# Latent attention: the value products of both key halves in one run per four heads

## The reference, cut to what matters

```
q = (x @ Wq + bq).reshape(B, S, H, Dh)
latent = x @ Wl + bl
k = (latent @ Wk + bk).reshape(B, S, H, Dh)
v = (latent @ Wv + bv).reshape(B, S, H, Dh)
scores = jnp.einsum('bihd,bjhd->bhij', q, k) * SCALE
attn = jax.nn.softmax(scores, axis=-1)
out = jnp.einsum('bhij,bjhd->bihd', attn, v).reshape(B, S, D)
out = out @ Wo + bo
```

## Time and profile before

| what | value |
|---|---|
| median of 3 runs | 912.23 us (909.99 to 913.12) |
| profiled execution, its own time | 912.18 us |
| its span, first to last instruction | 910.4 us |
| TensorE busy, share of the span | 88% |
| latent stage, turns 0 to 7 | 513.9 to about 661 us of the span |

### The profile page before, as it was taken

One profiled execution on the slowest core, in us unless ns is written; L12 is line 12 of the kernel. 1 busy time (PEld: TensorE's weight loads), 2 busy tenths in 40 slices (PEclk: granted clock), 3 DMA queues, 4 the chain that ended last, 5 costly groups with the idle time before them and its releaser, 6 DMA issues.

```text
span 910.4 us, 22033 instructions
## 1 busy us (share of the span) xinstructions
PE 798.7 (88%) x8648; PEld 535.8 (59%) x8648; DVE 588.9 (65%) x1662; ACT 404.0 (44%) x993; POOL 177.7 (20%) x355
## 2 busy tenths in 40 slices
PE   2579999976599999999985899999959999998997
PEld 1445555535366667668862455555536666667885
DVE  5847878866646776775654566667444677676564
ACT  2435444424244444434431266667614444443443
POOL 6105434521100100000003554331000000000000
PEclk9979999977799999999995599999979999999998
DMA  6000000000000000000002322232000000000000
GB/s 214 0 1 1 2 1 1 2 1 0 0 1 3 2 3 2 2 3 1 1 2 73 101 76 85 84 85 63 2 1 1 3 3 3 2 2 2 2 25 24
DMA packets 13764, 20.01 MB, mean 22 GB/s; under 512 B 1504, under 2 KB 12128, under 8 KB 12256
## 3 DMA queue, kind: packets, MB, share of 16 engines
q1 hardware_dynamic: 13520, 18.43, 6.9%
q10 hardware_dynamic: 144, 0.20, 0.1%
HBM read 14.30 MB, written 4.19 MB: 20 GB/s over the span
## 4 chain that ended last, share of the span: by engine, by line
PE 74%; DVE 11%; issue 5%; ACT 5%; POOL 3%; DMA 1%; DVEq 0%; SPq 0%; ACTq 0%; POOLq 0%
PE bank L1624 8%; PE bank L1696 7%; PE bank L1682 5%; PE bank L1666 5%; PE bank L1631 3%; PE bank L1722 3%; PE bank L1105 3%; PE bank L617 2%; PE bank L1886 2%; PE bank L1126 2%; PE bank L1139 2%; PE bank L1840 2%; PE bank L1827 2%; PE bank L629 2%; PE bank L1835 1%
## 5 line engine op out<-in xcount | busy, mean ns | idle before, releaser
L1422 DVE TENSOR_REDUCE arena<-bank 128x2 f32<-128x512 f32 x128 | 85.1, 688 | 53.4 <-PE bank L1105 53.1
L1243 ACT ACTIVATE arena<-bank 128x512 f32<-128x512 f32 x128 | 74.5, 594 | 51.2 <-PE bank L1126 50.4
L2214 DVE TENSOR_REDUCE arena<-bank 128x4 f32<-128x768 f32 x64 | 61.2, 956 | 32.1 <-PE bank L1666 32.1
L1624 PE MATMUL bank<-arena,w_sb 128*128 128x256 f32 x256 | 75.9, 422 | 1.3 <-ACT arena L1962 1.3
L1983 ACT ACTIVATE arena<-bank 128x768 f32<-128x768 f32 x64 | 51.9, 811 | 44.2 <-PE bank L1688 44.2
L2123 POOL TENSOR_TENSOR arena<-arena,c_sb 128x8 bf16<-128x8 f32 x32 | 9.0, 280 | 286.8 <-issue 249.2
L1682 PE MATMUL bank<-arena 64*64 64x192 f32 (+1 forms) x1024 | 54.9, 308 | 0.4 <-ACT arena L1983 0.4
L1696 PE MATMUL bank<-arena 128*32 128x192 f32 x1024 | 53.9, 328 | 1.6 <-DVE x L2229 1.6
L1624 PEld LDWEIGHTS bank<-arena,w_sb 128*128 128x128 f32 x256 | 46.2, 200 | 14.7 <-ACT arena L1962 2.1
L1105 PE MATMUL bank<-arena 72*128 72x256 bf16 x256 | 52.6, 293 | 1.1 <-DVE arena L1422 1.1
L1126 PE MATMUL bank<-arena 128*128 128x256 bf16 x256 | 49.8, 278 | 0.5 <-ACT arena L1243 0.4
(11 more groups left out here) (297 smaller groups left out, 1793.7 us busy)
## 6 DMA issues: line engine op xcount, KB each, us to landing
arena<-q_dram SPq DMA_DIRECT2D x24, 192.0 KB
arena<-k_dram SPq DMA_DIRECT2D x24, 192.0 KB
w_sb<-w_dram SPq DMA_DIRECT2D x2, 1514.5 KB, 10.3
q_dram<-arena SPq DMA_DIRECT2D x24, 64.0 KB, 2.8
k_dram<-arena SPq DMA_DIRECT2D x24, 64.0 KB, 2.0
x<-x_dram SPq DMA_DIRECT2D x4, 256.0 KB, 4.6
out_dram<-x SPq DMA_DIRECT2D x4, 256.0 KB, 2.3
arena<-arena SPq DMA_DIRECT2D x32, 4.0 KB
```

Source lines behind the costliest of these rows:

```text
L1243: act.activation(a_pT[:, u % (2 * GROUP), :, :].rearrange("p k t -> p (k t)"), bank[2 + u % 2][:, :], ACT.Exp).then_inc(S["p"], 1)
L1422: dve.tensor_reduce(a_mx[:, i % 2, :, u % GROUP], bank[s % 2][:, :].rearrange("p (h k) -> p h k", h=HALVES), AX_X, ALU.max, negate=True).t ...
L1624: ins = pe.matmul(to[:, j * T:(j + 1) * T], w_sb[:, at:at + P], g_zT[b % 2][:], start=True, stop=True)
L2214: dve.tensor_reduce(g_mx[:, s, :, :, i].rearrange("p h j -> p j h"), two_banks(0)[:, :, 0:SPAN].rearrange("p j (h k) -> p j h k", h=HALVES ...
```

## The change

Before, a run stands at every odd step: at steps 1, 5, 9 and 13 the first half of the keys of a group, and two steps later, at 3, 7, 11 and 15, the second half. (A group's runs come five and seven steps after its first head, so those of the last group of a batch stand in steps 1 and 3 of the next turn.) After, both halves stand at steps 1, 5, 9 and 13, one behind the other, and nothing stands at the other odd steps. The products are the same in number and form.

```diff
                     at = b * AH + u - GROUP - 1
-                    if u % 2 == 1 and 0 <= at < B * AH:
-                        values(at // AH, at % AH // GROUP, at % GROUP // 2)
+                    if u % GROUP == 1 and 0 <= at < B * AH:
+                        for k in range(HALVES):
+                            values(at // AH, at % AH // GROUP, k)
```

## The result

The changed kernel takes 924.5 us (median of 4 runs, 922.98 to 925.49) against 912.12 for the kernel before (912.23 in the runs shown ahead, one more was added). The ratio is 1.0137, with a 95% interval of 1.0115 to 1.016. I had forecast 919.6 and a range up to 923.5: the direction was right, the loss of 12.4 us lies outside the range.

A forecast was written before the change was run, and what follows sets the result against it. TensorE's list was taken to set the pace, other engines counting only where it waits. Turn losses of 0.86 + 3.66 + 0.86 + 0.9 + 1.1 = 7.4 us on 912.2 gave 919.6 us, range 914.5 to 923.5.

The forecast's parts named there:

- What a run and a second run cost: On TensorE, a run of `values` taken away frees 0.66 us; a second run right behind another adds 0.43.
- The chains: Within a turn, each second run delays the next chain's start by 0.43 us; freed 0.66 mostly becomes waiting; +1.22 at turn end.
- The sum: Latent stage, turns 0 to 7: 0.86 + 3.66 + 0.86 + 0.9 + 1.1 = 7.4 us lost.
- the three waits: TensorE's waits before `turn_outputs` of step 7, `project_out` and `turn_y`, forecast to grow to about 0.9 to 1.1 us.
- the sentence on the bounds: Latent stage: waits growing to some 0.9 us could cost clock; no row shows longer ones; only a little chance left.
- the prediction's own signs of being wrong: Waits staying at 0.2 to 0.5 us, two runs not following at 0.43, or granted clock leaving 1.00 inside the stage.
- The first: Rival: TensorE keeps the drains saved because chains have slack, 905.1 us; faster, below 909.5, had chance 0.07.
- The second: Rival: delays of steps 13 and 9 not handed on, 914.9 us or about 912; 909.5 to 917 had chance 0.13.
- The third: Rival: second run costs 0.58 us, or a GpSimd chain comes late, 924.3 us; 922 to 927 had chance 0.10.

## Why the prediction was right in its mechanism and wrong in its size

- **What a run and a second run cost** (0.66 and 0.43): measured 0.41 for the second, and 0.43 where the transposes stand ahead of both (from turned scores to scores 1.38 us, 574.37 to 575.75, against the 0.95 above). Right.
- **The chains.** `turn_outputs`, `project_out` and `turn_y` later by 0.36 to 0.43 each, `project_kv` by 0.07 earlier, a middle turn longer by 1.22. Measured one by one +0.43 (step 5), +0.38 (9), +0.41 (13), −0.10 (1), together +1.15. Right, and the kernels with one pair show that the freed time is lost in the chains, place by place.
- **The sum** of 7.4 us. Without the falls of the clock it was 7.25: with the three waits filled the stage is 155.88 us against 148.63. Turn by turn 0.86 was forecast and 0.87 measured for turn 0 (20.17 against 19.30), 1.22 and 1.15 for the middle ones, 0.86 and 0.81 for turn 4 (20.81 against 20.00), 0.45 and 0.55 for turns 5 and 6, 1.1 and 1.03 for turn 7 (18.34 against 17.31).
- **The step that failed** is the sentence on the bounds: "Waits that grow to some 0.9 could cost clock ... so I leave a little chance to it". It named the mechanism, and the sum priced it at nothing. That the clock leaves 1.00 inside the stage stood among the prediction's own signs of being wrong, and it came. Three falls of 3.4 us at half the clock cost 160.61 − 155.88 = 4.7 us in the profiled execution, 1.6 each. Over all executions it is some 5.5 us (a loss of 12.4 against one of 6.85). The three others of the changed kernel took 924.47 to 925.49 us at a mean granted clock of 0.930 to 0.934, the profiled one 922.98 at 0.935, so they probably had more falls; no trace of them was kept. Nor do the traces tie the falls to a wait of 0.9: all came behind one of 0.74 to 0.76, and `turn_y` alone waited 1.12 without one. The loss was 12.4 and not 7.4.
- **What I could have seen.** The prediction itself said that three waits would grow to between 0.9 and 1.1 in each middle turn (they became 0.76 to 1.12), and that no row showed the clock at such waits. A bound without a row should have gone into the range with a price: at 1.6 us a fall, three of them would have taken its upper end beyond 923.5.
- **The rivals.** The first, that the drains saved are kept (905.1), did not hold. Its saving is real (TensorE is busy for 17.94 and not 18.57 us of a turn), but it turned into waiting. The second, slack behind steps 9 and 13, did not hold either: with the halves together there alone a middle turn lost 0.38 and 0.41. The third, a second run at 0.58, is refuted by the 0.41 to 0.43, and among TensorE's waits of the changed stage none is for GpSimd; that its 924.3 lies near the measured time is chance.

## What to carry to other kernels

Work that stands right in front of an instruction that waits anyway costs nothing there, as the idle products showed (a turn of 21.26 against 21.25). Moved ahead of the work that starts this wait's chain, it costs its full time (0.38 to 0.43 here), even if the move saves the engine something. So before work is put together, look at each place for what it covers and for which chain begins behind the new place. And when waits grow on a TensorE that was dense until then, put a price on the clock into the range; whether it falls can be tested by filling the waits with idle products.

## What was not expected of the hardware

- Idle stretches of under a microsecond were enough for the granted clock to go to 0.50 for 3.4 us now and then. All five falls in the traces came 1.5 to 2.6 us behind a `project_out` that had waited 0.74 to 0.76, and in turn 6, of the changed kernel and of that with step 9 alone, it was the only long wait. The same wait in other turns had no fall behind it, so what decides it stays open.
- Transposes with 8 result rows cost 0.06 us beside a run of products with 32 result rows and 0.29 alone between scores and turned scores. Whoever moves the one should count the other.
